# Two layers of modulated attention and experts on one core: the first layer's filler work regrouped on all engines, and two subtractions of the first attention moved ahead

## The reference

```python
# layer 0
h = _layernorm(x) * (1 + ca) + sa
Q = einsum('bnd,kd->bnk', h, W_Q); K = einsum('bnd,kd->bnk', h, W_K)
M = einsum('bnk,bnd->bkd', K, h)
J_new = einsum('bnk,bkd->bnd', Q, M) / sqrt(128) + h
x = x + ga * (_layernorm(J_new) * gamma + beta)
h = _layernorm(x) * (1 + cb) + sb
x = x + gb * moe(h)        # 8 experts 128->512->128, top 2, gelu
# layer 1
h = _layernorm(x) * (1 + ca) + sa
x = x + ga * attention(h)  # 16 heads, softmax over 64 anchors for each token
h = _layernorm(x) * (1 + cb) + sb
x = x + gb * ffn(h)        # 128 -> 512 gated, 512 -> 512 twice, 512 -> 128
```

## Time and profile before

| | |
|---|---|
| median of 3 runs | 786.03 us (785.18 to 786.83) |
| profiled execution, its own time | 785.84 us |
| its span | 784.1 us |
| PE, DVE, ACT, POOL busy | 84%, 73%, 51%, 35% of the span |

### The profile page before, as it was taken

How to read it: one execution, slowest core, us unless ns; L and a number is a source line. 1 busy time by engine, 2 the same in 40 slices (tenths; PEclk the granted TensorE clock), 3 DMA queues, 4 the chain that set the end, 5 groups by cost and what they waited for, 6 DMA issues and landing times.

```text
span 784.1 us, 9644 instructions
## 1 busy us (share of the span) xinstructions
PE 656.5 (84%) x2985; PEld 474.0 (60%) x2985; DVE 570.3 (73%) x1443; ACT 400.9 (51%) x698; POOL 271.5 (35%) x227
## 2 busy tenths in 40 slices
PE   5577841199999995679989899999899899899897
PEld 3467731178888874345468656468555478556575
DVE  4988767568877746976977686976786866793763
ACT  3455443167777742325276444375444485452573
POOL 6346767400000016687202276202475220341100
PEclk9896655589999995889999999999999999999999
DMA  5631277778899721000000000000100000000000
GB/s 210 206 101 45 108 277 288 252 254 266 268 280 337 229 80 31 23 21 20 8 1 0 34 21 28 1 0 1 37 24 22 0 1 1 27 1 1 0 1 28
DMA packets 25780, 69.26 MB, mean 88 GB/s; under 512 B 5297, under 2 KB 8385, under 8 KB 24385
## 3 DMA queue, kind: packets, MB, share of 16 engines
q1 hardware_dynamic: 21632, 60.24, 22.3%
q0 software_dynamic: 4096, 8.40, 3.4%
HBM read 46.46 MB, written 22.16 MB: 88 GB/s over the span
## 4 chain that ended last, share of the span: by engine, by line
PE 61%; DVE 21%; issue 5%; ACT 4%; POOL 4%; DMA 3%; SPq 1%; DVEq 0%; ACTq 0%; POOLq 0%
PE ps L1657 15%; PE ps L1653 9%; PE ps L1659 8%; PE ps L1661 6%; PE ps L1660 6%; PE ps L1913 6%; DVE stats L1051 3%; POOL rows_by_expert L601 2%; PE ps L1901 2%; PE ps L1931 2%; DVE lsum L1506 2%; PE ps L1703 2%; DVE ring L1538 2%; DMA raw<-in_w 1%; DVE yb L1438 1%
## 5 line engine op out<-in xcount | busy, mean ns | idle before, releaser
L642 POOL DMA_INDIRECT yb<-y_by_expert,ypos x64 | 63.8, 997 | 158.3 <-DMA y_by_expert<-ysb 142.6
L1657 PE MATMUL ps<-hid,fh 128*128 128x512 f32 x256 | 103.3, 404 | 5.1 <-DVE hid L1522 5.1
L1659 PE MATMUL ps<-hid,fh 128*128 128x512 f32 x256 | 101.4, 396 | 0.0
L690 POOL TENSOR_TENSOR misc<-misc,ring 128x1024 f32<-128x1024 f32 x28 | 66.0, 2356 | 35.5 <-DVE ring L1512 30.4
L601 POOL DMA_INDIRECT rows_by_expert<-h,pos x64 | 68.9, 1076 | 25.3 <-issue 18.5
L1522 DVE TENSOR_TENSOR hid<-ring,hid 128x512 fp32r<-128x512 f32 x56 | 38.6, 689 | 41.3 <-ACT hid L930 39.7
L1657 PEld LDWEIGHTS ps<-hid,fh 128*128 128x128 f32 x256 | 48.1, 188 | 20.9 <-DVE hid L1522 10.4
L1913 PE MATMUL ps<-ring,hn 128*128 128x512 f32 x112 | 55.4, 617 | 5.0 <-DVE ring L1512 5.0
L1931 PE MATMUL ps<-attnT,cmat 128*128 128x512 f32 x128 | 56.9, 593 | 0.0
L987 ACT ACTIVATE ring<-ps 128x1024 f32<-128x1024 f32 x32 | 32.8, 1024 | 44.2 <-PE ps L1901 44.0
L1659 PEld LDWEIGHTS ps<-hid,fh 128*128 128x128 f32 x256 | 48.2, 188 | 10.5
(11 more groups left out here) (323 smaller groups left out, 1681.2 us busy)
## 6 DMA issues: line engine op xcount, KB each, us to landing
wbuf<-w_split SPq DMA_DIRECT2D x46, 512.0 KB, 5.4
w_split<-parts SPq DMA_DIRECT2D x4, 2048.0 KB, 7.0
raw<-in_w SPq DMA_DIRECT2D x8, 512.0 KB, 8.9
xs<-rows_by_expert SPq DMA_DIRECT2D x16, 256.0 KB, 5.6
y_by_expert<-ysb SPq DMA_DIRECT2D x16, 256.0 KB, 4.8
ffn_raw<-in_ffn SPq DMA_DIRECT2D x1, 2816.0 KB, 11.2
rows_by_expert<-zeros SPq DMA_DIRECT2D x9, 256.0 KB, 2.3
xa<-in_x SPq DMA_DIRECT2D x4, 512.0 KB, 6.3
```

What stands on the lines that cost most here:

```text
L642: gp.indirect_dma_start(yb[:, k, t, :], None, ydisp, bass.IndirectOffsetOnAxis(ypos[:, b, k, t:t + 1].bitcast(U32), 0))\
L690: gp.tensor_tensor(asum, asum, ring[:, 2 * (t % 2):2 * (t % 2) + 2, :] .rearrange("p a n -> p (a n)"), ALU.add).then_inc(*pool_asum.raise_(t))
L1657: te.matmul(out_, w(0), x(0), start=first, stop=False)
L1659: return te.matmul(out_, w(0), x(1), start=False, stop=last_)
```

## The change

- SP: x of batch 0 is loaded ahead of the first wmod half, x of batch 1 ahead of the second.
- Statistics are cut in two: `tile_stats` (bn_stats) and `aggregated`; batch 2 has a buffer of its own, `next_stats`. The bn_stats of batches 1 and 2 and the sums of batches 2 and 3 come earlier in DVE's order.
- The two remainders of weight group 0 go from DVE to POOL, behind the first half of zb; POOL's roots are reordered around them.
- ACT makes z of batch 2 before zb of batch 0, and z of batch 3 right after h1 of batch 0 (it was in batch 1's turn).
- DVE's `centred(1)` and the `modt` copies, `inner_stats(1)`, statistics of batch 3, the constants and `onehot` change places; `residual_1` and PE's `jn_centred` of batch 1 are cut into halves; PE's gates wait for each half of h1T by itself, and its transposes of z(2) follow the ranks.
- In the second layer's attention of batch 0, DVE's subtraction for hTa of spans 2 and 3 comes ahead of `sums` and `scaled`.

```diff
@@ -178,6 +178,7 @@
 stats = sb("stats", [128, T, 6])
+next_stats = sb("next_stats", [128, T, 6])
 LNS = ("L0a", "L0i", "L0b", "L1a", "L1b")
@@ -295,7 +296,9 @@
 pool_beta = sem("pool_beta")
-w_hi, w_lo = Once(sem("w_hi"), range(4)), Once(sem("w_lo"), [(q, i) for q in range(4) for i in range(2)])
+w_hi, w_lo = Once(sem("w_hi"), range(4)), Once(sem("w_lo"), [(q, i) for q in range(1, 4) for i in range(2)])
+pool_lo = Once(sem("pool_lo"), [(0, i) for i in range(2)])
 f_hi, f_lo = Once(sem("f_hi"), range(4)), sem("f_lo")
@@ -458,8 +461,9 @@
     load(silu[:, :], ins["cT"], l_mod)
+    load(xa[:, 0], by_tile(ins["x"][0]), l_x[0])
     load(wm[:, 0, :], ins["wmod"][:, 0:768], l_mod)
-    load(xa[:, 0], by_tile(ins["x"][0]), l_x[0])
+    load(xa[:, 1], by_tile(ins["x"][1]), l_x[1])
     load(wm[:, 1, :], ins["wmod"][:, 768:1536], l_mod1)
@@ -467,7 +471,7 @@
         load(dst, src, l_small)
-    for b in range(1, B):
+    for b in range(2, B):
         load(xa[:, b], by_tile(ins["x"][b]), l_x[b])
@@ -486,7 +490,7 @@
     for q in range(4):
-        sp.wait_ge(*w_lo.done((q, 1)))
+        sp.wait_ge(*(w_lo if q else pool_lo).done((q, 1)))
         load(wsplit[2 * q:2 * q + 2].rearrange("e p n -> p e n"),
@@ -624,11 +628,17 @@
     rstd("L0i", 0)
-    rstd("L0b", 0)
+    rstd("L0a", 2)
     pool.wait_ge(l_rows, 16)
...
     gp.tensor_tensor(xa[:, 1], xa[:, 1], over_tiles(R_GBETA, 1, T), ALU.add).then_inc(pool_beta, 1)
-    rstd("L0a", 2)
+    rstd("L0b", 0)
+    pool.wait_ge(*zb_done(0, 0))
+    pool.wait_ge(*w_hi.done(0))
+    for i in range(2):
+        gp.tensor_tensor(parts[0][:, :, i, 1, :], raw[0][:, i], f(parts[0][:, :, i, 0, :]), ALU.subtract)\
+            .then_inc(*pool_lo.raise_((0, i)))
     rstd("L0i", 1)
@@ -814,6 +824,7 @@
     first_half(1)
+    z_made(2)
     act.wait_ge(*dve_setup.done("modt"))
@@ -821,8 +832,8 @@
             h1_out(b, g)
-        if b + 2 < B:
-            z_made(b + 2)
+        if b == 0:
+            z_made(3)
         tanh(b)
@@ -1045,15 +1056,20 @@
-    def norm_stats(own, k, at_, srcs):
-        n = len(srcs)
+    def tile_stats(own, srcs, to=stats):
         for i, s in enumerate(srcs):
-            last = v.bn_stats(stats[:, i, :], s)
+            last = v.bn_stats(to[:, i, :], s)
         settle_alone(own, last)
+    def aggregated(own, k, at_, n, of=stats):
         for i in range(n):
-            last = v.bn_aggr(mv[k][:, at_ + i, :], stats[:, i, :])
+            last = v.bn_aggr(mv[k][:, at_ + i, :], of[:, i, :])
         settle(own, last)
         return v.tensor_scalar(ve[k][:, at_:at_ + n], mv[k][:, at_:at_ + n, 1], EPS, None, ALU.add)
+    def norm_stats(own, k, at_, srcs):
+        tile_stats(own, srcs)
+        return aggregated(own, k, at_, len(srcs))
@@ -1098,9 +1114,16 @@
-    def first_stats(b):
+    def first_stats(b, to=stats):
         dve.wait_ge(l_x[b], 16)
-        norm_stats("rows", "L0a", 0, [xa[:, b, t, :] for t in ts]).then_inc(*dve_var["L0a"].raise_(b))
+        tile_stats("rows", [xa[:, b, t, :] for t in ts], to)
+    def first_sums(b, of=stats):
+        if b:
+            dve.wait_ge(*dve_nmr["L0a"].done(b - 1))
+        if b == 1:
+            dve.wait_ge(*z_done(0, 0))
+        aggregated("rows", "L0a", 0, T, of).then_inc(*dve_var["L0a"].raise_(b))
@@ -1132,18 +1155,19 @@
-    def residual_1(b):
-        if b == 1:
+    def residual_1(b, halves=gs2):
+        if b == 1 and 0 in halves:
             dve.wait_ge(pool_beta, 1)
-        if b < POOL_ROOTS["L0i"]:
+        if b < POOL_ROOTS["L0i"] and 0 in halves:
             dve.wait_ge(*pool_rs["L0i"].done(b))
-        for g in gs2:
+        for g in halves:
             dve.wait_ge(*pe_jn.done((b, g)))
...
             last.then_inc(*dve_x1.raise_((b, g)))
-        dve.wait_ge(*dve_x1.done((b, 1)))
+        if 1 in halves:
+            dve.wait_ge(*dve_x1.done((b, 1)))
@@ -1280,10 +1304,12 @@
     first_stats(0)
+    first_sums(0)
     dve.wait_ge(*pe_setup.done("cols0"))
...
     v.tensor_copy(modt[:, :, SA0], pt[:, :, 1]).then_inc(*dve_setup.raise_("modt0"))
+    first_stats(1)
     norm_ready("L0a", 0)
@@ -1291,7 +1317,8 @@
     v.tensor_copy(ones_r[:, :], ones_f[:, :]).then_inc(*dve_setup.raise_("consts"))
-    first_stats(1)
+    first_sums(1)
+    first_stats(2, next_stats)
@@ -1315,7 +1342,11 @@
     inner_stats(0)
-    remainders(0, 0)
+    first_sums(2, next_stats)
+    residual_1(0)
+    minus_mean("L0a", 2)
+    second_stats(0)
+    centred(1)
@@ -1326,38 +1357,33 @@
     settle("setup", v.tensor_copy(jv[:, :], ps[:, 6, 128:160]))
-    residual_1(0)
-    second_stats(0)
+    norm_ready("L0b", 0)
+    half_normalized("L0b", zb, "zb")
     v.tensor_scalar(order[:, :], jv[:, 0:E], -1.0, float(E), ALU.mult, ALU.add)
     v.tensor_scalar(erow[:, :], jv[:, 0:E], float(REGION), None, ALU.mult)
-    v.tensor_scalar(thr[:, :], jv[:, 0:E], float(GW), None, ALU.mult)
-    v.tensor_scalar(tot[:, :], jv[:, 0:E], 0.0, None, ALU.mult)
-    settle("setup", v.tensor_scalar(unit[:, :], jv[:, 0:NT], 0.5, WIDE / 2.0, ALU.mult, ALU.add))
-    v.tensor_tensor(unit[:, :], unit[:, :], jv[:, 0:NT], ALU.min)
-    v.tensor_tensor(upto[:, :, :], jv[:, 0:2 * E].unsqueeze(1).broadcast_to([128, 2 * E, 2 * E]),
-                    jv[:, 0:2 * E].unsqueeze(2).broadcast_to([128, 2 * E, 2 * E]), ALU.is_le)\
-        .then_inc(*dve_setup.raise_("jv"))
+    v.tensor_scalar(tot[:, :], jv[:, 0:E], 0.0, None, ALU.mult).then_inc(*dve_setup.raise_("jv"))
+    inner_stats(1)
+    first_stats(3)
+    first_sums(3)
     dve.wait_ge(*dve_setup.done("jv"))
-    remainders(0, 1)
-    norm_ready("L0b", 0)
-    half_normalized("L0b", zb, "zb")
-    centred(1)
-    v.tensor_copy(onehot[:, :], oh_f[:, :])
-    first_stats(2)
-    inner_stats(1)
...
-    norm_ready("L0a", 2)
     choose(0)
-    first_stats(3)
+    minus_mean("L0a", 3)
+    residual_1(1, (0,))
     positions(0)
-    residual_1(1)
-    norm_ready("L0a", 3)
+    residual_1(1, (1,))
     second_stats(1)
     norm_ready("L0b", 1)
+    v.tensor_scalar(thr[:, :], jv[:, 0:E], float(GW), None, ALU.mult)
+    settle("setup", v.tensor_scalar(unit[:, :], jv[:, 0:NT], 0.5, WIDE / 2.0, ALU.mult, ALU.add))
+    v.tensor_tensor(unit[:, :], unit[:, :], jv[:, 0:NT], ALU.min)
+    settle("setup", v.tensor_tensor(upto[:, :, :], jv[:, 0:2 * E].unsqueeze(1).broadcast_to([128, 2 * E, 2 * E]),
+                                    jv[:, 0:2 * E].unsqueeze(2).broadcast_to([128, 2 * E, 2 * E]), ALU.is_le))
     for b in range(1, B):
@@ -1379,6 +1405,7 @@
     y_positions()
+    v.tensor_copy(onehot[:, :], oh_f[:, :])
@@ -1584,20 +1611,21 @@
         neg_max(3, b)
+        if b == 0:
+            hT_attn(2, 0)
         sums(2, b)
...
         if b == 0:
-            hT_attn(2, 0)
             combine(0, 3)
...
                 normalized("L1a", 3, 0)
+            if b == 0 and t == 5:
+                hT_attn(3, 0)
             sums(t - 1, b)
             scaled(t - 1, b)
-            if b == 0 and t == 5:
-                hT_attn(3, 0)
@@ -1711,9 +1739,9 @@
-    def jn_centred(b):
+    def jn_centred(b, halves=gs2):
         pe.wait_ge(*dve_pcat.done(b))
-        for g in gs2:
+        for g in halves:
             if b:
@@ -1728,10 +1756,11 @@
     def gates(b):
-        pe.wait_ge(*act_h1T.done((b, 1)))
         if b:
...
         for t in ts:
+            if t % GT == 0:
+                pe.wait_ge(*act_h1T.done((b, t // GT)))
             last = te.matmul(ps[:, 6, t * E:(t + 1) * E],
@@ -1793,12 +1822,12 @@
     product(1)
+    jn_raw(1)
     for g in gs2:
         zb_transposed(0, g)
-    jn_raw(1)
+    jn_centred(1, (0,))
     pe.wait_ge(*dve_setup.done("jv"))
     gates(0)
-    jn_centred(1)
     for b in bs:
@@ -1811,10 +1840,10 @@
         if b == 0:
-            z_transposed(2, 0)
+            jn_centred(1, (1,))
         ranks(b)
         if b + 2 < B:
-            for g in gs2[1 - min(b, 1):]:
+            for g in gs2:
                 z_transposed(b + 2, g)
```

## The result

The changed kernel took 776.64 us, the median of six runs (775.87 to 780.26), against 786.43 for the kernel before beside it (783.06 to 787.64); the ratio is 0.9886, 95% interval 0.9866 to 0.9907, so 9.0 us faster, with 7.3 to 10.5 as its bounds. Forecast were 777.0. The profiled execution is the slowest of the six: 780.26 us with a span of 778.5.

What follows compares the result with a forecast made beforehand. The first stage was taken as bound by POOL's scatters waiting for DVE's positions, batch 0's second attention by DVE-POOL lock and waits. First stage 0.6 + 1.6 + 2.8 = 5.0, attention 4.0: 9.0 us, giving 777.0, range 774 to 780.

Steps and rivals of the forecast that it cites:

- 1.6 + 2.8: First stage, batches 1 to 3: DVE's waits for batch 2's raw product (1.6 us) and batch 3's product (2.8) go.
- Part 1: First stage up to the start of zb: gain 0, bounds -1 to +2; the 2.3 us stall moves to nmr, costing 1.8.
- slow ranks of batch 0: Before the first scatter: TensorE idles four microseconds ahead of the ranks, runs at 0.50, costing 0.9 us more.
- the cap of 5.9 us: First stage: POOL's packed scatters limit the gain to 5.9 us of waits plus the first scatter's gain.
- The 0.6 us: From zb to the first scatter: forecast gain 0.6 us, range 0.4 to 3.4, with the tensor_scalar held by POOL's subtractions.
- The 2.8 us: Batch 3 in the first stage: z made ahead on ACT removes DVE's 3.0 us wait, taken as +2.8.
- Second place: Attention of batch 0: PE resumes 3.9 us sooner, DVE's 4.23 us wait goes; maximum 5.3 earlier in all.
- A: Rival: DVE-POOL lock eats the first stage with two more holds, one more in the attention; 782.0 us, chance 0.20.
- B: Rival: no collisions between DVE and POOL; first stage gains 7.8, attention 5.3; 773.0 us, chance 0.18.
- D: Rival: POOL's sums set the attention's pace, its gain nearly nil (0.5 us); 780.5 us, chance 0.06.
- E: Rival: slower, POOL's subtractions and roots wait behind DVE, so the first scatter comes late; 788.5 us, chance 0.05.
- F: Rival: nothing gained, both gains given back at a later wait, weights or gathers; 786.0 us, chance 0.05.

Runs made afterwards that it cites:

- beta_behind: Changed kernel with POOL's addition of beta to batch 1 waiting for DVE's small nmr of batch 2; 804.57 us, 0.9880 of the kernel before on that chip.
- sub_on_dve: Changed kernel with weight group 0's two subtractions put back from POOL on DVE, after batch 1's second normalization; 804.21 us, 0.9845 of the kernel before.
- z3_again: Changed kernel with batch 3's normalized rows made one batch later on ACT, run on the last chip; 779.76 us, changed kernel beside it 779.14.
- z3_late: Changed kernel with batch 3's normalized rows made one batch later on ACT, run on the slower chip; 811.45 us, 0.9938 of the kernel before.
- attn_first: Kernel before with only the first attention subtraction (third tile group's) moved ahead of sum and product; 811.82 us, 0.9977 of the kernel before.
- head_only: Changed kernel with both attention moves undone, only the regrouped first stage left; 811.99 us, 0.9960 of the kernel before.

## Why the prediction was right

The total of 9.0 us was met to the decimal, and that is luck. The first stage gave 5.8 us for a forecast 5.0, the attention 2.6 for 4.0, and 0.6 of the timed gain lie in neither. Inside the first stage the first scatter gave 1.1 us more than forecast and POOL's idle time 1.5 more (5.9 for 1.6 + 2.8), and scatters that grew by 2.2 us, which stand in no term of the sum, took most of it back. The mechanisms of the two stages are those that the prediction names; the sizes are off, and the errors cancel.

**Where it agrees.** Part 1's stall moved as forecast: nmr held 1.71 us (forecast 1.8) from 30.08 (30.3). The tensor_scalar was held 2.08 us (2.1). The Trainium skill (SBUF — State Buffer, "SBUF: two separate sides") calls the shared port pair an exclusive lock; the rows agree, and `beta_behind` and `sub_on_dve` show the price. Batch 2's raw product came to full clock: 1.74 us for the forecast 1.6, and TensorE's 4.12 us idle ahead of it are 0.74. The slow ranks of batch 0 came too: TensorE stood 4.29 us ahead of them, was granted 0.50, and DVE waited 0.94 us (forecast 0.9). POOL's packing took the stage over, at the cap of 5.9 us that the prediction states: positions came 8.5 us earlier for batch 3 (114.37, for 122.85), the expert rows 5.8.

**First scatter: mis-sized.** The 0.6 us were 1.7. Half of zb came at 36.16, a microsecond earlier than "0" for part 1 allowed, so POOL's subtractions, and with them the end of the hold, came at 42.0 and not at 43.2.

**Batch 3: size about right, cause open.** The 2.8 us were put on z(3), made early on ACT. The wait of 3.0 us went, and the next positions moved by another 3.3 us (7.2 earlier for batch 2, after 3.9 for batch 1). Two things can have done it. One is z(3); the other is TensorE's clock, with a Gram matrix of 2.02 us for 3.62 and shorter matmuls ahead of it. No run has either alone against the kernel before. On the last chip `z3_again` (late z, full clock) and the changed kernel (early z, half clock from 66 to 70) both lack the wait, so there neither an early z nor a clock that stays up all the way is needed; `z3_late` (late z, half clock) has it, at 4.7 us. The prediction named only z(3), and counted the clock for batch 2's product alone. What moved the clock is open as well: that the closed gap did it is argued, and the changed kernel's second profile speaks against it. In time `z3_again` and the changed kernel don't differ (0.0 us, plus or minus 2.4), and in both POOL's scatters of batches 2 and 3 start without a wait.

**Attention: 4.0 forecast, 2.6 measured.** The steps to the seventh tile were right: 1.8 us at the fifth (2.1 forecast), 5.0 in all at the seventh (5.3). The give-back was sized 1.3 and is 2.4: the casts of tiles 6 and 7 take 2.77 and 1.02 us, where 0.17 is the length of a free one. And "Second place" credited the second move with the larger half of the 5.3; `attn_first` reaches the seventh tile as early without it (33.06, for 32.97), and in the end the second move is worth nothing, or minus 0.5.

**The rivals.** A needed two more holds ahead of the first scatter: there is none, but one hold stood where no rival looked, on POOL's own scatter (5.83 us; taking it away brought the experts 1.8). The other half of A, one more hold in the attention for 1.5 us, is near what happened there. B's 773 needed no collisions; with both taken away by hand, the first scatter came at 48.1, and the gain was stopped by the next bound, DVE's positions. D (an attention gain of 0.5) is too low by 2 us, and of E and F, a late first scatter and a gain given back whole, nothing is seen.

## What to carry to other kernels

Where two engines share a lock and run two loops side by side, an earlier instruction is worth what it does to the meetings of the long ones: a 3 us wait that overlaps a partner's operation can be cheaper than the order that removes it. When a chain's waits are gone, look at what the engine that issues the last step is packed with, and then at its DMA's landing: a hold of 4.9 us taken away here gave 1.8. And before a gain is put on a piece of work done earlier, compare the lengths of the same matmuls in both profiles: here three groups alone were 3.4 us shorter, and two executions of one kernel differ in the same way (2.03 and 3.76 us for one group).

## What the runs showed of the hardware

**DVE's subtractions hold POOL's indirect DMAs.** These, of 1 us, took 5.83 (in two profiles of the changed kernel), 5.84 (`z3_again`) and 7.19 us beside 6 us of two-input fp32 subtractions on DVE, over several of them in a row (each takes 0.7 to 2.3 us). In the kernel before the same subtractions let one in after 3.02 us. Beside pieces of 512 columns (0.7 us each, each waited for) none took over 1.15 us. In the attention POOL's gathers took 1.77 us for 0.96 beside DVE's products. The Trainium skill (the same page and section) tells of GpSimd's DMAs starved while DVE is in a two-port fast mode; here two-input fp32 operations do it.

**A chip on which engines stand still.** On the second chip ScalarE, TensorE and VectorE stood in the first stage with no releaser in the profile, while POOL issued scatters. ScalarE in `head_only`, whose transposes had ended at 61.8:

```profile
68.89 0.78 ACT L735 ACTIVATE h1T<-ps,modt 128x512 f32<-128x512 f32 x1 [7.77 <-remote]
73.85 0.78 ACT L735 ACTIVATE h1T<-ps,modt 128x512 f32<-128x512 f32 x1 [4.19 <-remote]
```

Gaps of up to 13.5 us with the releaser "remote" or "issue" stand in all eight traces of that chip, "remote" in no trace of the others before 180 us; the time was 28 us longer. The cause isn't in the traces and stays open. An experiment whose effect is in that stretch must be read against a run of its own base on the same chip.
